# A three-layer compressed interaction network on one Trainium2 core: two stores a unit, half units in front, an interleaved end, five group buffers and a ring of sixteen

## The reference

```python
x0 = e                                   # (B, 32, 16), gathered by ids
xk = x0
for W in (W0, W1, W2):
    xk = relu(einsum('bmd,bhd,mhk->bkd', x0, xk, W))
    outs.append(sum(xk, axis=2))
h = concat(outs + [dense_ctx])
y = relu(relu(h @ W_top1 + b_top1) @ W_top2 + b_top2) @ W_top3
```

## Time and profile before

| what | us |
|---|---|
| median of three runs (lowest, highest) | 680.91 (677.95, 681.98) |
| the profiled execution, its own time | 675.9 |
| its span, first to last instruction | 674.0 |
| mean granted TensorE clock | 0.967 |

### The profile page before, as it was taken

One profiled execution on the slowest core, in us unless ns is written; L12 is line 12 of the kernel. 1 busy time (PEld: TensorE's weight loads), 2 busy tenths in 40 slices (PEclk: granted clock), 3 DMA queues, 4 the chain that ended last, 5 costly groups with the idle time before them and its releaser, 6 DMA issues.

```text
span 674.0 us, 7501 instructions
## 1 busy us (share of the span) xinstructions
PE 572.9 (85%) x2472; PEld 191.5 (28%) x2472; DVE 558.0 (83%) x231; ACT 317.5 (47%) x1311; POOL 461.0 (68%) x353
## 2 busy tenths in 40 slices
PE   0047599989989898989898989898998989895997
PEld 0002132333323232323232323232333423231332
DVE  0039798989999999999899999999998999996400
ACT  0031447364555646454646473746456464643031
POOL 5776484977878887878697979788887873443000
PEclk9998699899999899989999999999898999997999
DMA  3296685776757576767586777777685667570000
GB/s 91 65 353 218 261 300 230 271 286 254 298 223 298 223 248 253 255 256 283 214 301 241 276 282 273 285 270 287 244 311 201 248 241 309 206 243 0 1 0 0
DMA packets 32918, 153.35 MB, mean 228 GB/s; under 512 B 11600, under 2 KB 21584, under 8 KB 24816
## 3 DMA queue, kind: packets, MB, share of 16 engines
q1 hardware_dynamic: 22656, 149.31, 57.6%
q0 software_dynamic: 8192, 2.11, 2.6%
q10 hardware_dynamic: 2032, 1.46, 0.7%
HBM read 147.61 MB, written 5.25 MB: 227 GB/s over the span
## 4 chain that ended last, share of the span: by engine, by line
PE 52%; DVE 21%; DMA 11%; issue 6%; ACT 5%; SPq 3%; POOL 2%; ACTq 0%; DVEq 0%
PE acc L484 47%; DVE prod L341 19%; DMA spread<-x_scratch 6%; DMA x_scratch<-xt 4%; ACT x L392 4%; SPq L205 3%; POOL rows L295 2%; PE x L553 2%; PE x L542 1%; DVE z L353 1%; DVE xt L331 1%; DMA first<-x_scratch 1%; PE x L559 1%; PE x L546 0%; PE acc L542 0%
## 5 line engine op out<-in xcount | busy, mean ns | idle before, releaser
L341 DVE TENSOR_TENSOR prod<-spread,x 128x4096 f32<-128x4096 f32 (+2 forms) x179 | 531.1, 3022 | 47.7 <-ACT x L392 20.4
L484 PE MATMUL acc<-prod,w 128*64 128x512 f32 x1932 | 453.7, 617 | 95.1 <-DVE prod L341 89.5
L295 POOL DMA_INDIRECT rows<-table,idx x256 | 242.7, 948 | 79.0 <-issue 70.4
L307 POOL TENSOR_TENSOR prod_pool<-spread,x_pool 128x1024 f32<-128x1024 f32 x93 | 218.1, 2374 | 84.3 <-ACT x_pool L392 84.1
L484 PEld LDWEIGHTS acc<-prod,w 128*64 128x64 f32 x1932 | 147.8, 141 | 389.5 <-issue 351.7
L392 ACT ACTIVATE x<-acc 64x512 f32<-64x512 f32 x128 | 73.0, 570 | 79.0 <-PE acc L484 77.8
L407 ACT ACTIVATE relu_out<-acc 128x512 f32<-128x512 f32 x48 | 28.7, 597 | 157.3 <-PE acc L484 156.5
L400 ACT ACTIVATE relu_out<-relu_out 128x16 f32<-128x16 f32 x480 | 95.3, 200 | 0.5
L484 PE MATMUL acc<-prod_pool,w 128*64 128x512 f32 x372 | 90.9, 592 | 0.0
L400 ACT ACTIVATION_READ_ACCUMULATOR relu_out<-relu_out 128x1 f32 x480 | 89.8, 187 | 0.0
L392 ACT ACTIVATE x_pool<-acc 64x512 f32<-64x512 f32 x128 | 75.7, 591 | 1.9
(11 more groups left out here) (20 smaller groups left out, 26.9 us busy)
## 6 DMA issues: line engine op xcount, KB each, us to landing
spread<-x_scratch SPq DMA_DIRECT2D x63, 2048.0 KB, 9.3
first<-x_scratch SPq DMA_DIRECT2D x16, 512.0 KB
rows<-table,idx POOLq DMA_INDIRECT x256
x_scratch<-xt SPq DMA_DIRECT2D x64, 48.0 KB
spread<-x_scratch SPq DMA_DIRECT2D x4, 512.0 KB, 8.2
x_scratch<-xt SPq DMA_DIRECT2D x60, 32.0 KB
w<-w ACTq DMA_DIRECT2D x2, 512.0 KB, 5.7
spread<-wt SPq DMA_DIRECT2D x2, 384.0 KB, 4.4
```

The source lines that it names most:

```text
L295: nc.gpsimd.indirect_dma_start(rows[u % 2][:, j * D:(j + 1) * D], None, table, bass.IndirectOffsetOnAxis(ap=idx[:, u, j:j + 1], axis=0)).t ...
L307: nc.gpsimd.tensor_tensor(prod_pool[:, k % POOL_SLOTS, :], tiles(u, t, 1)[:, 0, :], x[:, :], ALU.mult).then_inc(pool_ready, 1)
L341: nc.vector.tensor_tensor(prod[:, at:at + count, :], tiles(u, t, count), x[:, :].rearrange("p (a n) -> p a n", a=1).to_broadcast([P, count ...
L484: last = nc.tensor.matmul(to[K * blk:K * blk + K, :], w, moving[:, blk * BLK:(blk + 1) * BLK], start=start, stop=stop)
```

## The change

The 1024 samples go in 17 units: two *half units* of 32 samples (`HALVES`), then 15 of 64; `LAST` is 16. Unit u from 2 on stands where unit u-1 stood. In a half unit every tile, load and matmul has 512 columns.

The gather takes 32 samples x four quarters of the fields, so a half unit needs 8 indirect DMAs and a full one 16; the ids come rearranged from the host in two loads. The columns of a tile now lie as four runs, each of two halves of 128: the turn leaves a field's row as four partitions in a row, and a unit is stored with two DMAs, one of all 128 partitions twice and one of the first 44 partitions (75 rows in all, 80 before). Matmuls, `spread_out` and the sums read and write in four runs of 128 columns (`side`, `parts`). SyncE makes all stores; in the first unit, ScalarE made half of them.

`spread` has five group buffers, `prod` sixteen products. Group g of unit u takes buffer (4u+g) mod 5: group 0 of unit u+1 waits for step 3 of layer 3 of unit u-1, groups 1, 2 and 3 for steps 0, 1 (with GpSimd's tile 7) and 2 of layer 3 of unit u. The sum of x1 of unit u lies after layer 1 of u+1, ahead of the wait for x2. At the end, three steps of layer 3 of unit 15, then layer 2 of unit 16, then the last step of layer 3 of unit 15, then layer 3 of unit 16, whose x2 goes where x0 and x1 for GpSimd were. Layers 2 and 3 of unit 0 and layer 2 of unit 1 have no tiles on GpSimd. The tower's weights fit into one group buffer, which that last step of unit 15 releases. ScalarE loads its table with a small ACTIVATE ahead of the first unit. `bank_of` waits for the accumulator's previous stage, as the waits before did.

```diff
-UNITS = 16
-S = B // UNITS
+S = 64
...
-F = 2
-J = M // F
-ROWS = 3 * M
-RING = 12
-BUFFERS = 6
+J = 8
+ROWS = 2 * M + 11
+RING = 16
+BUFFERS = 5
...
+
+HALVES = 2
+UNITS = HALVES + (B - HALVES * S // 2) // S
+LAST = UNITS - 1
+COLS = B // 2
...
-    return () if (layer, u) == (2, 0) else (5, 6, 7)
+    return () if (layer, u) in ((2, 0), (3, 0), (2, 1)) else (5, 6, 7)
...
+    second = 1 if pool_tiles(layer, u) else 4
     if layer == 2:
-        return (0, 2), (2, 2), (4, 4 if u == 0 else 1), (8, 4), (12, 2), (14, 2)
-    return (0, 4), (4, 1), (8, 4), (12, 4)
+        return (0, 2), (2, 2), (4, second), (8, 4), (12, 2), (14, 2)
+    return (0, 4), (4, second), (8, 4), (12, 4)
...
+CUT = 3
+CUT_ORDER = ([("step", 0), ("step", 1), ("pool", 0), ("pool", 1), ("step", 2), ("pool", 2)], [("step", 3)])
+
+
...
+    yield from every(3, LAST - 1)[:CUT]
+    yield from every(2, LAST)
+    yield from every(3, LAST - 1)[CUT:]
+    yield from every(3, LAST)
...
-        def store(engine, u, f):
-            times = 3 - f
-            for g in range(2):
-                for c in range(2):
-                    to = scratch[u, J * f, g * BLK + c * (BLK // 2)]
-                    to = bass.AP(tensor=to.tensor, offset=to.offset, ap=[[N, J], [M * N, times], [1, BLK // 2]])
...
-                    engine.dma_start(to, src.to_broadcast([J, times, BLK // 2])).then_inc(scratch_in[u % 2], 16)
...
+        def store(engine, u):
+
+            n = width(u) // 4
+            to = scratch(u, 0)
+            to = bass.AP(tensor=to.tensor, offset=to.offset, ap=[[n, P], [M * 4 * n, 2], [1, n]])
+            src = xt[u % 2][:, 0:n].rearrange("p (a n) -> p a n", a=1)
+            engine.dma_start(to, src.to_broadcast([P, 2, n])).then_inc(scratch_in[u % 2], 16)
+            to = scratch(u, 2 * M)
+            to = bass.AP(tensor=to.tensor, offset=to.offset, ap=[[n, 4 * (ROWS - 2 * M)], [1, n]])
+            engine.dma_start(to, xt[u % 2][0:4 * (ROWS - 2 * M), 0:n]).then_inc(scratch_in[u % 2], 16)
+
+        def side(x, blk):
+
+            return x.rearrange("p (c g n) -> p g c n", c=4, g=2)[:, blk, :, :]
+
+        def parts(x):
+
+            return x.rearrange("p (c n) -> p c n", c=4)
...
-            store(sp, 0, 0)
+            store(sp, 0)
...
-            load_group(0, 1)
-            sp.wait_ge(tile_in[3], 16)
-            load_group(0, 2)
-            sp.wait_ge(*loaded(0, G))
-            load_group(0, 3)
-            for u in range(UNITS - 1):
+            for g in range(1, GROUPS):
+                load_group(0, g)
+            for u in range(LAST):
                 sp.wait_ge(turned, u + 2)
-                for f in range(F):
-                    store(sp, u + 1, f)
+                store(sp, u + 1)
                 load_first(u + 1)
 
-                if u >= 1:
-                    sp.wait_ge(prod_ready, made(3, u - 1, 2))
-                load_group(u + 1, 0)
                 if u >= 1:
                     sp.wait_ge(prod_ready, made(3, u - 1, 3))
-                load_group(u + 1, 1)
+                load_group(u + 1, 0)
                 sp.wait_ge(prod_ready, made(3, u, 0))
                 sp.wait_ge(square_ready, u + 1)
+                load_group(u + 1, 1)
+                sp.wait_ge(prod_ready, made(3, u, 1))
+                if pool_tiles(3, u):
+                    sp.wait_ge(pool_ready, POOL_PLACES[3, u, 2] + 1)
                 load_group(u + 1, 2)
-                sp.wait_ge(prod_ready, made(3, u, 1))
-                sp.wait_ge(pool_ready, POOL_PLACES[3, u, 2] + 1)
+                sp.wait_ge(prod_ready, made(3, u, 2))
                 load_group(u + 1, 3)
...
             for g in range(2):
-                sp.dma_start(out.rearrange("(u g b) o -> g o u b", g=2, u=UNITS)[g],
-                             y[:, g, :].rearrange("p (u b) -> p u b", u=UNITS)).then_inc(stored, 16)
-            sp.wait_ge(stored, 32)
+                sp.dma_start(out[S:B, :].rearrange("(u g b) o -> g o u b", g=2, b=S // 2)[g],
+                             y[:, g, S // 2:COLS].rearrange("p (u b) -> p u b", b=S // 2)).then_inc(stored, 16)
+                sp.dma_start(out[0:S, :].rearrange("(u g b) o -> g o u b", g=2, b=S // 4)[g],
+                             y[:, g, 0:S // 2].rearrange("p (u b) -> p u b", b=S // 4)).then_inc(stored, 16)
+            sp.wait_ge(stored, 64)
...
+                for j in range(fields(u))[part]:
+                    group = u if half(u) else HALVES + 2 * (u - HALVES) + j // J
+                    index = ids_sb[:, group - 1, j % J:j % J + 1] if group else ids0_sb[:, 0, j:j + 1]
...
-                                        relu_out[layer][:, :].rearrange("p (e b d) -> p b e d", e=2, d=D // 2),
...
+                                        relu_out[layer][:, 0:n].rearrange("p (c b e) -> p b c e", c=4, e=D // 4),
...
-            for u in range(UNITS):
+            turn(1)
+            for u in range(LAST):
                 dve.wait_ge(x_ready[0], u + 1)
                 for i in range(len(steps_of(2, u))):
                     multiply(2, u, i, x1)
-                    if u == 0 and i == 2:
-                        turn(1)
-                if u == 0:
-                    sum_d(0, 0)
-                if u + 1 < UNITS:
-                    layer_1(u + 1)
+                layer_1(u + 1)
+                sum_d(u, 0)
                 dve.wait_ge(x_ready[1], u + 1)
-                for i in range(len(steps_of(3, u))):
-                    if i == 3 and u + 2 < UNITS:
-                        turn(u + 2)
-                    multiply(3, u, i, x2)
-                    if i == 2:
-                        sum_d(u, 1)
-                if u + 1 < UNITS:
-                    sum_d(u + 1, 0)
-            sum_d(UNITS - 1, 2)
+                if u + 1 < LAST:
+                    for i in range(len(steps_of(3, u))):
+                        if i == (2 if u == 0 else 3) and u + 2 < UNITS:
+                            turn(u + 2)
+                        multiply(3, u, i, x2)
+                        if i == 2:
+                            sum_d(u, 1)
+            for i in range(CUT):
+                multiply(3, LAST - 1, i, x2)
+            sum_d(LAST - 1, 1)
+            dve.wait_ge(x_ready[0], LAST + 1)
+            for i in range(len(steps_of(2, LAST))):
+                multiply(2, LAST, i, x1)
+            sum_d(LAST, 0)
+            for i in range(CUT, len(steps_of(3, LAST - 1))):
+                multiply(3, LAST - 1, i, x2)
+            dve.wait_ge(x_ready[1], LAST + 1)
+            for i in range(len(steps_of(3, LAST))):
+                multiply(3, LAST, i, x2_of(LAST))
+                if i == 1:
+                    sum_d(LAST, 1)
+            sum_d(LAST, 2)
 
         @block.scalar
         def _(act):
-            def spread_out(to, src):
+            def spread_out(u, to, src):
+                n = width(u) // 2
                 for blk in range(2):
-                    for half in range(2):
-                        last = nc.scalar.activation(to[K * half:K * half + K, blk * BLK:(blk + 1) * BLK],
-                                                    src[K * blk:K * blk + K, :], ACT.Relu)
+                    for copy in range(2):
+                        last = nc.scalar.activation(side(to[K * copy:K * copy + K, 0:2 * n], blk),
+                                                    parts(src[K * blk:K * blk + K, 0:n]), ACT.Relu)
                 return last
...
-            act.wait_ge(turned, 1)
-            store(act, 0, 1)
+
+            act.wait_ge(consts_in, 48)
+            nc.scalar.activation(warm[:, :], w_sq[0:1, 0:1], ACT.Relu)
...
-            for u in range(UNITS):
-                if u + 1 < UNITS:
-                    base_tile(u + 1)
-                    if u:
-                        squares(u + 1)
+            for u in range(LAST):
+                base_tile(u + 1)
+                if u:
+                    squares(u + 1)
                 after_2(u)
-                if u + 1 < UNITS:
-                    after_1(u + 1)
-                after_3(u)
-                if u + 1 < UNITS:
+                after_1(u + 1)
+                if u + 1 < LAST:
+                    after_3(u)
                     sum_3(u)
+            after_2(LAST)
+            after_3(LAST - 1)
+            sum_3(LAST - 1)
+            after_3(LAST)
...
                 for blk in range(2):
-                    last = nc.tensor.matmul(to[K * blk:K * blk + K, :], w, moving[:, blk * BLK:(blk + 1) * BLK],
+                    last = nc.tensor.matmul(parts(to[K * blk:K * blk + K, 0:n]), w, side(moving[:, 0:2 * n], blk),
                                             start=start, stop=stop)
...
-            for u in range(UNITS):
-                layer(u, 2)
-                if u + 1 < UNITS:
-                    layer_1(u + 1)
-                layer(u, 3)
+            for u in range(LAST):
+                layer(u, 2, order_of(2, u))
+                layer_1(u + 1)
+                if u + 1 < LAST:
```

(68 more changed lines are left out.)

228 lines of the change are left out of this document (111 added, 117 removed).

## The result

The change makes the kernel slower: 729.92 us median of four runs (723.52 to 736.07) against 679.43 (673.23 to 681.98), a ratio of 1.073 with an interval of 1.061 to 1.084. The profiled execution took 729.94 us, its span is 728.1 and the mean granted clock 0.922.

What follows compares the result with a forecast made beforehand. Before: a loop of VectorE, TensorE and ScalarE; after: SyncE's queue of loads and stores. Front 109, 13 units x 39.4 and end 93 make 714.2; with 1.9 outside and 5.0 carried, 721 us, range 688 to 757.

Steps and rivals of the forecast that it cites:

- The loop of queued loads: Steady units: groups 1 to 3, stores, `first`, group 0 queue on SyncE; layer 3 every 38.7 us instead of 35.3.
- The allowance for late units: Steady units: 0.7 us a unit for late group 0, from 10.1 us over 15 units; 38.7 becomes 39.4.
- The front: Start to layer 3 of unit 2: 109 us, before 114.97; only 6 of 12 us gained, bounds 104 to 115.
- half groups land in 2.7 steps: Front: landing step for half-size groups; unit 1's group 0 lands near 41, its layer 1 ends near 43.5.
- The end: From layer 3 of unit 15 to the end: 93.0 us, before 93.7; layer 3 of unit 16 at T+32.9.
- The ring: Sixteen products: VectorE waits for a free one once, 0.3 us; costed at nothing, at best giving those 0.3.
- the strided columns: Matmuls, ScalarE's copies and sums in four runs of 128 columns: no difference taken; 17.56 us for 80 matmuls unstrided.
- The sum of x1: VectorE, now last before layer 3: 0.6 us a unit, hidden before, now counted in the loop.
- The clock: Rival, slower still: TensorE's clock falls after each unit's stall, 2.7 us more, 42.1 a unit, 756 carried; chance 0.11.
- The sum: Whole span: 109 + 13 units x 39.4 + 93 = 714.2 us; 716.1 with 1.9 outside, 721 with 5.0 carried.
- The stores pass the loads: Rival, faster: SyncE's queue not in order, stores land about T+13.5, units back to 35.3, 663 us carried; chance 0.10.
- The queue at its best: Rival, same: landings that make 36.3 us a unit, total 674, 681 carried; chance 0.05.

Runs made afterwards that it cites:

- e3: The changed kernel, five buffers kept, with the stores of unit u+2 issued ahead of group 3 of unit u+1; 677.32 us, ratio 0.998 to the kernel before.
- e7: The changed kernel with the 64-row store issued twice, the second time into spare scratch rows that nothing reads; 740.95 us, ratio 1.087 to the kernel before.
- the four orders: Groups ahead of the stores, with `first` out: changed kernel 1 to 3, T+24.0; e1 2 and 3, T+19.05; e3 1 and 2, T+19.5; e5 2, T+14.0.
- e5: The changed kernel with six buffers, a ring of 12 and the stores issued ahead of group 3; 651.3 us, ratio 0.957 to the kernel before.
- e2: The changed kernel with only the ring of products back to 12, five buffers kept; 726.07 us, ratio 1.068 to the kernel before.
- e1: The changed kernel with six group buffers and a ring of 12 again, the rest of the change kept; 663.2 us, ratio 0.977 to the kernel before.
- e4: The changed kernel with the stores from unit 1 on issued on ScalarE's queue after x1, five buffers kept; 716.48 us, ratio 1.059 to the kernel before.
- e8: e4 with each group loaded as four one-tile DMAs, so load packets are 4 KB, not 16 KB; 688.3 us, ratio 1.011 to the kernel before.

## Why the prediction was right, step by step

**The loop of queued loads held.** In the unit with T = 316.20 group 1 landed at T+11.8 (forecast 11.9), group 3 at T+23.2 (22.7), `first` left at T+24.0 (24.4), layer 1 began at T+33.5 (33.7), the next layer 3 at T+38.45 (38.7). Two terms were off and partly cancelled: the groups landed 5.7 us apart, not 5.4, and from group 3's landing to `first` passed 0.8 us, not 1.7. That the stores' place decides, and their size little, is shown by e3 and e7, and the 5 us for each group ahead of them by the four orders. The limit near 358 GB/s of the Trainium skill, "DMA: Bandwidth & Descriptors", section "Where 436 GB/s comes from", would by the forecast's working have made the mean unit an estimated 43.2 us; it took 39.94. That working was itself wrong: it adds the difference from 423 GB/s to a sum whose step of 5.4 us for 2 MB is 388, and the 5.7 us measured are 368. So the units alone do not decide; the trace disagrees with the limit in the window 328:334, where 408 GB/s moved.

**The allowance for late units** was 0.7 and should have been 1.5 (39.94 - 38.45). It was taken from the gaps before, where only group 0 came late, and a gap shows no lateness below the 1.0 us that group 0 had in hand there (T+29.2 for T+30.2). In the slowest unit here group 3 took 15.0 us to landing and group 0 11.1.

**The front** was the worst term: 114.06, forecast 109. Its first step was right (22.49, forecast 23). What was wrong was "half groups land in 2.7 steps": that is how far apart queued ones would land, and I used it for a group 0 that comes alone. The one of unit 1 took 7.9 us to landing (the seven 1 MB groups 6.0 at the median), and unit 1's layer 1 began at 44.56, not 41. `first` of unit 2 went out at 61.17, not 58, and its group 0 took 10.7, not 8.7: layer 1 of unit 2 began at 72.55, behind a group 0 that I had near 68, and layer 3 of unit 1 at 77.21, not 72. From there on the forecast's steps fit: 37 us to layer 3 of unit 2, by it and by the trace. So the front kept 0.9 us of its head start, and e5's, with six buffers and the other order, keeps 15.9 (99.08 for 114.97): the queue ate the rest.

**The end** took 94.8, forecast 93.0. The terms in the forecast add to T+32.2 for layer 3 of unit 16, not to the T+32.9 written there. VectorE was indeed done at T+32.2, but then waited 1.63 us for its x2 and began at T+33.8, 0.9 late; what follows took the other 0.9 more.

**Costs put at nothing.** The ring cost nothing that e2 can tell. Nor did the strided columns on TensorE: 80 matmuls take 17.41 us in e5's chain, 17.56 before. The sum of x1 is hidden or not as the stall decides: with five buffers it stands in the loop of loads (0.6 a unit, counted), in e5 it lies beside the wait for x2 that follows it.

**The clock.** TensorE's timeline, and the windows 312:315.8, 315.8:320 and 320:324 of the kernel after (columns as in the earlier trace rows):
```profile
315.84 6.39 PE L586 MATMUL acc<-prod,w 128*64 128x512 f32 x16 [5.08 <-DVE prod L426]
```
```profile
312.00:315.80 3.80, 0.00 (x0) 0.00 (x0) 3.80 (x2) 3.72 (x8) 0.00 (x0) 0.84 0.03 2
315.80:320.00 4.20, 4.16 (x10) 1.40 (x12) 4.20 (x2) 1.70 (x3) 3.00 (x2) 0.50 0.01 2
320.00:324.00 4.00, 4.00 (x16) 1.07 (x14) 4.00 (x3) 0.71 (x2) 4.00 (x2) 0.83 0.52 197
```
TensorE stood idle for 5.08 us, to 315.84, and then ran at 0.50, its lower level of 1.2 GHz. So the rival's fall does happen in this unit; its price does not, since VectorE waits for x2 three times in all, 5.6 us, and never in a steady unit. The fall is hidden behind the wait for loads, as the forecast had it. The Trainium skill, "TensorE: Matmul & The Clock Gate", section "HAM oscillation — how this bites in real kernels", tells of a kernel that pays at each such wait; the trace shows the fall and no payment.

**The sum.** 5.1 of front, 13 x 0.54 = 7.0 of units and 1.8 of end make the span 13.9 longer than the 714.2 forecast. The median missed by only 8.9 because of the 5.0 carried from the median before: the median after stands at its profiled execution, 729.92 and 729.94. That carry was no property of the kernel: by luck it hid a third of the miss.

**The rivals.** "The stores pass the loads" fell: they waited for all three. It needed the stores through near T+13.5; `first` at T+14.0 is reached only by e5, with its order and its six buffers. "The queue at its best" wanted 36.3 a unit; no unit after is below 38.

## What to carry to other kernels

A small transfer on which the next load depends pays for the bulk loads issued ahead of it in the same queue, far more than for its own size: here 5 us for each 2 MB ahead, and some 0.6 for stores nearly twice as large. Before a buffer is given up, list what then waits behind the later loads in the queue, and issue the small dependent transfers ahead of the bulk; here that order alone gave back 53 us (e3), the buffer 67 (e1), and both together 79 (e5). Read a long wait's place off the timeline of the issuing engine, not off busy shares: both big engines lost share here while none was at fault.

## What the runs showed that I had not expected

A queue of its own did not free the small transfers: on ScalarE's queue the stores took 12 to 14.5 us to `first` (e4), hardly sooner than behind the loads (13.0, from 327.29 to 340.24), since their first packet moved 3.6 us after the issue, and then one 1 KB packet for one of 16 KB. The Trainium skill, "DMA: Bandwidth & Descriptors", section "Queues, rings and completion order", says that an engine turns from queue to queue packet by packet, a packet there holding several descriptors; the profile counts the two queues' packets one for one (20 and 20 in e4). With 4 KB loads the stores took 8.9 us (e8), 4.8 of them in such sharing; why their first packet comes so late after the issue was not settled.
